# Expert loop: contraction of 128 + 64 features instead of 2 x 96, and its prologue woven into the work before it

## The reference, cut to what matters

```python
h = tokenizer(x)                       # 32 images, 64 patches each, 192 features: ff, windowed attention, ff
h = concatenate([cls, h], axis=1)      # 65 rows per image, T = 2080 rows
h = h + attention_with_top_26_keys(layernorm(h))
x = layernorm(h).reshape(-1, 192)
sig = sigmoid(x @ Wg.T)                # E = 128 experts
topk_idx = top_k(sig + e_bias, 6)[1]   # 6 experts a row, capacity 192 rows an expert
xb = x[token_buf]                      # [expert, 192, 192]: the rows of each expert
g, u = split(einsum('ech,ehf->ecf', xb, W_gate_up), 2)   # 192 -> 2 x 464
yb = einsum('eci,eih->ech', silu(g) * u, W_down)         # 464 -> 192
routed = zeros.at[token_buf].add(yb * w_buf)
return h + routed + (silu(x @ Wsg) * (x @ Wsu)) @ Wsd    # the shared expert, 928 wide
```

## Time and profile before

| | us |
|---|---|
| median of 3 runs (962.62 to 972.72) | 965.27 |
| profiled execution | 968.73 |
| its span | 966.9 |
| woven part and ranks, until the list is ready | 0 to 705.9 |
| experts' loop, first product to last down product | 740.9 to 951.6 |

### The profile page before, as it was taken

How to read it: one execution, slowest core, us unless ns; L and a number is a source line. 1 busy time by engine, 2 the same in 40 slices (tenths; PEclk the granted TensorE clock), 3 DMA queues, 4 the chain that set the end, 5 groups by cost and what they waited for, 6 DMA issues and landing times.

```text
span 966.9 us, 22008 instructions
## 1 busy us (share of the span) xinstructions
PE 862.3 (89%) x7603; PEld 800.8 (83%) x7603; DVE 750.9 (78%) x3778; ACT 330.3 (34%) x931; POOL 284.1 (29%) x350
## 2 busy tenths in 40 slices
PE   1787799898999999989999999999975999999993
PEld 1677688798888888878899999998765999999993
DVE  4256898999999899999989796987653767666773
ACT  0235553553563654455354444321100111111110
POOL 6021212412430331241232311211102445445544
PEclk9999998999999999999999999999876999999997
DMA  7410010101001000100110000111004555645541
GB/s 203 123 49 1 2 41 6 37 17 38 28 27 31 20 27 19 31 27 18 33 41 28 8 17 25 38 29 40 23 5 102 141 129 122 145 113 131 126 109 24
DMA packets 43430, 52.57 MB, mean 54 GB/s; under 512 B 5733, under 2 KB 35883, under 8 KB 43308
## 3 DMA queue, kind: packets, MB, share of 16 engines
q1 hardware_dynamic: 37452, 45.25, 17.1%
q0 software_dynamic: 5888, 6.20, 3.9%
HBM read 41.31 MB, written 10.11 MB: 53 GB/s over the span
## 4 chain that ended last, share of the span: by engine, by line
PE 36%; DVE 31%; DMA 10%; issue 9%; POOL 6%; ACT 4%; SPq 3%; DVEq 0%; POOLq 0%; ACTq 0%
DVE b_arena L1486 7%; DMA out_rows<-b_hid,b_add_index 5%; DMA out_rows<-b_inner,b_add_index 4%; SPq L613 3%; PE p_small L704 3%; POOL out_rows L1771 3%; PE p_shared L848 3%; PE p_big L697 3%; PE p_shared L842 3%; PE p_big L731 3%; PE p_shared L843 3%; PE p_big L698 3%; DVE b_top_a L1472 2%; POOL b_arena L1752 2%; DVE b_top_b L1472 2%
## 5 line engine op out<-in xcount | busy, mean ns | idle before, releaser
L1007 PE MATMUL p_big<-b_xeT,b_arena 96*116 96x192 f32 x640 | 110.3, 332 | 0.6 <-ACT b_xeT L1174 0.6
L1007 PEld LDWEIGHTS p_big<-b_xeT,b_arena 96*116 96x116 f32 x640 | 107.4, 184 | 1.0 <-ACT b_xeT L1174 0.9
L1530 DVE TENSOR_TENSOR b_arena<-b_iota_b,b_slot 128x1152 bf16<-128x1152 bf16 (+1 forms) x46 | 85.3, 1858 | 7.3 <-issue 7.3
L1752 POOL DMA_INDIRECT b_arena<-x_rows,b_index x44 | 46.0, 1046 | 144.5 <-DVE b_index L1596 58.6
L697 PE MATMUL p_big<-b_xT,b_ff1a 128*128 128x128 f32 x384 | 77.6, 285 | 1.8 <-ACT b_xT L1030 1.7
L698 PE MATMUL p_big<-b_xT,b_ff1b 128*128 128x128 f32 x384 | 76.5, 282 | 0.0
L1682 POOL TENSOR_TENSOR b_arena<-b_kY,b_mask_k 64x256 f32<-64x256 f32 x16 | 11.2, 698 | 200.6 <-ACT b_kY L1055 200.6
L697 PEld LDWEIGHTS p_big<-b_xT,b_ff1a 128*128 128x128 f32 x384 | 61.1, 199 | 3.8 <-ACT b_xT L1030 3.4
L1030 ACT COPY b_xT<-p_small 128x256 f32<-128x256 f32 (+1 forms) x97 | 35.6, 376 | 81.2 <-PE p_small L688 80.9
L698 PEld LDWEIGHTS p_big<-b_xT,b_ff1b 128*128 128x128 f32 x384 | 60.7, 199 | 0.0
L731 PE MATMUL p_big<-b_arena,b_q_blk 128*128 128x256 f32 (+3 forms) x256 | 48.9, 334 | 8.7 <-ACT b_q_blk L1062 8.3
(11 more groups left out here) (365 smaller groups left out, 2546.1 us busy)
## 6 DMA issues: line engine op xcount, KB each, us to landing
b_arena<-in_w_gate_up SPq DMA_DIRECT2D x20, 696.0 KB
b_arena<-in_w_down SPq DMA_DIRECT2D x20, 336.0 KB
b_xp<-in_xp SPq DMA_DIRECT2D x16, 384.0 KB, 3.1
xT_rows<-b_xmT SPq DMA_DIRECT2D x16, 128.0 KB, 1.9
b_xT_late<-xT_rows SPq DMA_DIRECT2D x16, 128.0 KB, 2.1
h_rows<-b_h SPq DMA_DIRECT2D x16, 96.0 KB, 1.6
x_rows<-b_xm SPq DMA_DIRECT2D x32, 48.0 KB, 2.0
b_h_late<-h_rows SPq DMA_DIRECT2D x16, 96.0 KB, 1.9
```

What stands on the lines that cost most here:

```text
L1007: last = mm(big[r][0:SC, bank, j * CAP:(j + 1) * CAP], w_gu[s][:, k, c:c + SC], xeT[s][:, k, :], start=(k == 0), stop=(k == 1))
L1530: last = tt(hot[s][:, tiles, :], iota_b[:, None, :].to_broadcast([128, n, CAP]), slot[:, tiles, bass.ds(e, 1)].to_broadcast([128, n, CAP]) ...
L1752: G.indirect_dma_start(xg[s][:, h, :], None, x_rows[:, :], bass.IndirectOffsetOnAxis(index[s][:, h:h + 1], 0)).then_inc(S(f"gathered{s}"), 16)
```

## The change: what it does

**Contraction.** The 192 features of an expert are split as 128 + 64 instead of 96 + 96. The gathered row has 256 elements (`DX`): the 192 features and the last 64 once more, so that after the transposes these 64 stand on partitions 0 to 63 and also on 64 to 127. The last 64 rows of the weights are loaded so that gate's lie on partitions 0 to 63 and up's on 64 to 127. Each turn then has 8 products over 128 rows and 8 over 64 rows, the latter alternating between the upper and the lower half of the array. The products over 128 rows of both rounds come first, then those over 64 rows of both rounds. Each stored row of x takes two transfers instead of one, and each expert's weights five instead of three.

**Prologue.** `slots_of`, `gathered`, `indices_of`, `gather` and the first copy of `xeT` become turns of `ranks`, `gathers` and `first_rows` in the lists. The stores of the shared expert's results move from SP to ACT (`stores`), SP keeps the fetches (`fetches`). The lists of turns of all engines are new. The banks of PSUM in which the small results stand are dealt out anew.

```diff
-        xeT = two("xeT", [EK, 2, CAP])
-        w_gu, at = carve(at, EK, 2, 2 * I)
+        xeT = two("xeT", [128, 2, CAP])
+        w_gu, at = carve(at, DA, 2 * I)
+        w_gu_late, at = carve(at, 2 * DB, I)
...
-        x_rows = nc.dram_tensor("x_rows", [ROWS, D], f32).ap()
+        lists_bank, aux = [small[1], small[2]], [small[0], sh_bank]
+        x_rows = nc.dram_tensor("x_rows", [ROWS, DX], f32).ap()
...
+                    sp.dma_start(to[:, 0:D], rows).then_inc(S("x_stored"), 16)
+                    sp.dma_start(to[:, D:DX], rows[:, DA:D]).then_inc(S("x_stored"), 16)
...
-            sp.sem_inc(S("eup1"), 2)
+            sp.sem_inc(S("eup1"), 1)
...
-                    sp.dma_start(w_gu[s][:], gu).then_inc(S(f"w_loaded{s}"), 16)
+                    sp.dma_start(w_gu[s][:], gu[0:DA, :]).then_inc(S(f"w_loaded{s}"), 16)
+                    sp.dma_start(w_gu_late[s][0:DB, :], gu[DA:D, 0:I]).then_inc(S(f"w_loaded{s}"), 16)
+                    sp.dma_start(w_gu_late[s][DB:2 * DB, :], gu[DA:D, I:2 * I]).then_inc(S(f"w_loaded{s}"), 16)
...
+                yield "pick0"
+                slots_of(0, 1)
+                yield "pick1"
+                slots_of(1, 2)
+                yield "rows0"
+                gathered(0, 32, 1)
+                pe.sem_inc(S("eup1"), 1)
...
-            pe.wait_ge(S("acc_ready"), NT)
-            slots_of(0, 1)
-            slots_of(1, 2)
-            gathered(0, 32, 1)
...
                     for r in range(2):
                         pe.wait_ge(S(f"einner{r}"), v)
-                        for bank in range(2):
-                            for j in range(2):
+                        for j in range(2):
+                            for bank in range(2):
                                 c = bank * I + (2 * r + j) * SC
-                                for k in range(2):
-                                    last = mm(big[r][0:SC, bank, j * CAP:(j + 1) * CAP], w_gu[s][:, k, c:c + SC],
-                                              xeT[s][:, k, :], start=(k == 0), stop=(k == 1))
+                                mm(big[r][0:SC, bank, j * CAP:(j + 1) * CAP], w_gu[s][:, c:c + SC], xeT[s][:, 0, :],
+                                   start=(j == 0), stop=False)
+                    for r in range(2):
+                        for j in range(2):
+                            c = (2 * r + j) * SC
+                            for bank, rows in enumerate((slice(0, DB), slice(DB, 2 * DB))):
+                                last = mm(big[r][0:SC, bank, j * CAP:(j + 1) * CAP], w_gu_late[s][rows, c:c + SC],
+                                          xeT[s][rows, 1, :], start=False, stop=(j == 1))
                         last.then_inc(S(f"eup{r}"), 1)
...
+            def gathers():
+                yield "gather0"
+                pool.wait_ge(S("x_stored"), 64 * TILES + 64)
+                pool.wait_ge(S("cls_x_stored"), 32)
+                pool.wait_ge(S("zero_rows"), 32)
+                gather(0, 1)
+                yield "gather1"
+                gather(1, 2)
...
-        patches1 class_keys1*2 tokens1*5 patches2 tokens1*2 patches3 tokens1 patches4 tokens1*4 tokens2
+        patches1 class_keys1*2 tokens1*7 patches2 tokens1 patches3 tokens1*4 patches4 tokens2 second_ff1
```

599 lines of the change are left out of this document (298 added, 301 removed).

## The result

The changed kernel takes 1025.03 us (median, 1023.42 to 1030.6); the kernel before, on the same chip, 964.78. The ratio is 1.059 (95% interval 1.054 to 1.064): it is slower by 60 us, where 35 were forecast. The profiled execution has a span of 1022.7 us against 966.9.

The account below looks back on a forecast made before the run. Two equal chains, PE's own work and round 0 through ACT and DVE to down, were taken to bound the turn. Loop +55, prologue -15, start -5 gave +35 on 965.3: 1000 us, forecast's own range 985 to 1014, bottom set at 957.

Parts of the forecast that it names:

- Direction and mechanism: Experts' loop: round 0, tanh on ACT, DVE's chain and down set a longer turn; kernel slower by 35 us, chance 0.68.
- Side by side or in series: Experts' loop: whether the 64-row products overlap on the two array halves, 1.30 us, or run one after another, 2.60; leaned to series.
- my two cases: Turn of the experts' loop with clock falls: side by side 10.62 + 2.9 = 13.5 us, in series 11.27 + 1.9 = 13.2.
- The fall of the clock: Experts' loop: stretches without large products drop PE's clock in nearly every or most turns, each fall costing 2.9 us.
- The loop: Twenty experts' turns of 13.3 us each, 266 us in all: +55 us.
- The prologue: From the expert list to the first expert: 20.9 us instead of 35, a gain of 14 to 16, taken as 15.
- the rest of the shared expert lies beside it: Prologue: of the shared expert only the class rows' down product, 5.2 us, was counted in the 20.9 us.
- The start and the lists: Transposes of y go 5.2 us earlier, gain kept: -5 us, ends 0 and -8; the rest of the new lists not costed.
- a slower woven part: Sign of being wrong: the woven part after the start loses more than the start gained; no size given.

Follow-up runs that it names:

- r0_first: Changed kernel with each round's four 64-row products right behind that round's four 128-row products: 966.22 us, 1.000 of the kernel before.
- one_half: Changed kernel with all 64-row products on rows 0 to 63 of the array: 1028.33 us, 1.061 of the kernel before.
- fill: Changed kernel with five unused 128x192 products on PE each turn, between the six-column products and down: 975.68 us, 1.010 of the kernel before.
- start_old: Changed kernel with the patch product of tile 2 back ahead of the transposes of the first tile's y: 1029.83 us, 1.067 of the kernel before.
- before_index_first: Kernel before (96 + 96 rows) with both compares behind the index and the scatters' landing awaited ahead of the next scatters: 957.79 us, 0.992.
- before_start: `before_index_first` with the patch product of tile 2 moved behind the first tile's transposes of y, queries, keys and values: 972.24 us, 1.003 of the kernel before.
- series: Changed kernel with a round's 64-row products ordered gate, gate, up, up instead of alternating between halves: 1023.69 us, 1.060 of the kernel before.
- index_first: `ring` with the first compare on DVE moved behind the five small steps of the index: 959.39 us, 0.993 of the kernel before.
- before_ring: Kernel before (96 + 96 rows) with the compare behind round 1 and the scatters' landing awaited ahead of the next scatters: 968.19 us, 1.003.
- both: `r0_first` with the first compare of a turn also moved behind round 1 on DVE: 973.05 us, 1.009 of the kernel before.
- ring: `both` with POOL's wait for the scatters' landing moved ahead of the next expert's scatters: 972.05 us, 1.005 of the kernel before.

## Why the prediction was right and wrong

**Direction and mechanism: right.** The turn is tanh, DVE's chain and down. It was forecast at 13.3, with a wait of 1 to 2 us for DVE's round 1 ahead of down, down products of 5.4 us and a clock well under 0.9 in the loop; it is 13.65, with 1.94, 5.41 and 0.75. `r0_first`, which only makes round 0 complete earlier, gives all of it back.

**Side by side or in series: wrong leaning, from a row read wrongly.** The 64-row products take 1.49 us, and `one_half` shows what series is, 2.85. I leaned to series by the earlier trace rows, where 10.7 us of busy time over 120 instructions gave 0.089 each. But that busy time holds the draining of each group, which lies under the next one. The starts tell it, in the timeline of the kernel before:

```profile
315.92 0.34 PE L721 MATMUL p_small<-b_wv1b,b_xT 128*64 128x96 f32 x4
316.08 0.34 PE L721 MATMUL p_small<-b_wv1a,b_xT 128*64 128x96 f32 x4
```

Four instructions with 96 columns, on two column places, are 0.16 us from start to start, 0.041 each. On the whole array two instructions with 128 columns are 0.22 apart (314.94 and 315.16 in that view), which is 0.083 for 96 columns. So the column places worked side by side as well, and the trace that I had could have told me. It did not change the size much, since my two cases came to 13.5 and 13.2 a turn.

**The fall of the clock: right in kind and, by luck, in price.** I priced it at 2.9 in nearly every turn; a turn pays 2.54 in down and 0.3 at the head of the next, in every turn but the first, which pays in part. `fill` measures 2.83. The 2.9 was the mean of 4.04 and 1.75, and neither was a whole fall alone: the first holds 1.1 us of a late gather, the second is a fall in which down took 4.50 and not 5.41. The Trainium skill, TensorE: Matmul & The Clock Gate, section "A second HAM failure mode", tells of a clock that swings because the engine idles briefly between groups of products; `fill` agrees, with 49 us won by closing the gap.

**The loop: +61 where I had +55.** The chain at full clock is 10.82, not 10.62: the 16 instructions over 128 rows take 2.70 us from start to start (2.60 forecast), the first 8 over 64 rows 0.75 (0.65). The other 0.2 a turn is that I took 13.3, between the two cases, when the case that held stood at 13.5.

**The prologue: this term failed, -15 forecast, -10.6 measured from the list on.** The step that failed is "the rest of the shared expert lies beside it". It does not. The gather itself kept to the forecast: the transfers of the first expert's rows ended at 726.6, 14.6 us after the list, where my terms give 14.8. But after the first index product PE does three rounds of the class rows' up products, one ahead of the second index product and two behind it. Each takes 3.09 us at the lower clock (719.05 to 722.14), 9.3 in all. So PE reaches the transposes only at 731.05, 4.4 after the rows had landed. The order shown ahead of the prediction has these rounds. I had counted the down product there and not the ups. The gain itself is steady: from the list to the first expert it is 24.5 to 26.1 us in all traces with the new prologue, 33.0 to 35.2 in all with the old one.

**The start and the lists: the largest single error, a term set at nothing.** The forecast had -5 for the start, and `start_old` measures 4.8. There is luck in this: the 5.2 was read from an execution in which the patch product took 3.76 us and the transposes of `y` came at 46.60. In the three other traces of the old lists with the old start it took 2.22, and they came at 43.5 to 43.7. The move as such brings them forward by 3.3 us (`start_old` against the changed kernel) or 2.9 (`before_index_first` against `before_start`). The step that failed is that the forecast kept this gain up to the list and set the rest of the new lists at nothing, because I could not cost them. They cost 11 us in this pair of traces: with them the list is 6 us later, in spite of the 5 gained at the start. Why the tiles turn more slowly with them is open.

**Sum of the errors:** lists 11, prologue 4.5, loop 6, end -1: 21 with rounding, on the profiled executions (+55.8 against +35). The other 4 us is the choice to predict from a median that lay 3.5 below the profiled execution.

**The range** ended at 1014, with 13.6 a turn and 12 for start and prologue. The turn was at its end, and the gains were 4 (10.6 less 6.3) where the range had at least 12; bad cases of the three terms were not added up, and a slower woven part had no case of its own, though I named it as a thing that would make me wrong.

## What to carry to other kernels

When products are split so that an engine ends sooner, look first at which of them completes the piece that the next engine waits for: order by consumer, not by kind of product. And price PE's saved microseconds at zero until the trace shows that the clock survives the hole they leave; here five unused products a turn won 49 us. A busy time divided by a count overstates the price of one instruction where groups overlap: take the distance of starts. A rewritten order for four engines is a change of its own: compare it by the pace of the steady stretch, which small terms at its ends do not tell.

## What the hardware showed

- Two sets of 64-row float32 products on the two row halves run side by side: 16 instructions in 1.49 us instead of 2.85 (`one_half`), and about as fast where each half's come in twos (1.65 with draining, `series`).
- A change between 128-row and 64-row products has a small price. At full clock the 32 instructions take 4.64 us in `r0_first`, in four groups (837.45 to 842.09), and 4.26 in `fill`, in two (833.91 to 838.17): two changes of kind more for 0.4 us.
- How long PE goes without large products does not tell by itself whether the clock falls. In `index_first` the ten turns in which 2.2 to 2.3 us passed from the end of the last 64-row product to down were slow, and the others, with 1.9, were not. With 96 + 96 rows in `before_ring` nine turns had 2.1 to 2.4, and eight of them kept the clock; in the kernel before two turns with 2.4 to 2.5 kept it. What else decides, the kind of products ahead or where in time the stretch lies, is open.
- A compare of 1.36 us that stands ahead of the five steps of 0.16 for which a gather waits can cost more than it did between the rounds: taken out of the chain it made `both` 7 us slower than `r0_first`, and put behind the steps it made `index_first` 13 us faster than `ring` and `before_index_first` 10 faster than `before_ring`.
